# VectorE's order in the expert stage of a decoder layer: the copy of a step's results stands elsewhere in its loop

## The reference

```python
logits = x @ gate_w.T
topv, topi = jax.lax.top_k(logits, TOP_K)          # TOP_K = 8 of 64 experts
rw = softmax(topv)
W = zeros((N, E)).at[arange(N)[:, None], topi].set(rw)
gate, up = split(einsum('nh,eih->nei', x, gu_w))   # inner size 64
inter = silu(gate) * up
out = einsum('nei,ehi->nh', inter * W[:, :, None], dp_w)
out = out + sigmoid(x @ sh_gate1_w.T) * shared_expert(x)
x = layernorm(x + out)
```

## Time and profile before

| | |
|---|---|
| median of three runs | 1790.8 us (1788.66 to 1800.23) |
| profiled execution, its own time | 1814.37 us |
| profiled execution, its span | 1812.6 us |
| mean granted TensorE clock in it | 0.943 |
| scatters in the span | 320, 321.9 us of GpSimd |
| copies of a sparse step's results | 160, 110.2 us of VectorE |

### The profile page before, as it was taken

One profiled execution on the slowest core, in us unless ns is written; L12 is line 12 of the kernel. 1 busy time (PEld: TensorE's weight loads), 2 busy tenths in 40 slices (PEclk: granted clock), 3 DMA queues, 4 the chain that ended last, 5 costly groups with the idle time before them and its releaser, 6 DMA issues. The chain is left out here.

```text
span 1812.6 us, 34769 instructions
## 1 busy us (share of the span) xinstructions
PE 1506.2 (83%) x9744; PEld 1232.2 (68%) x9744; DVE 1258.4 (69%) x3827; ACT 685.8 (38%) x1526; POOL 1052.3 (58%) x1023
## 2 busy tenths in 40 slices
PE   4799999999999889989899864887877778777596
PEld 3687878888787778878788753565555555555454
DVE  3788888888888888888888844455555555333387
ACT  3444444343444434434353412232222332222264
POOL 3557666676767667667676742555555555555421
PEclk8899999999999999999999976988899999989898
DMA  7513231322222121111211394655555655554596
GB/s 260 160 56 103 81 105 67 109 75 94 90 87 99 47 77 51 66 65 46 75 53 64 91 307 139 201 174 166 174 174 171 187 170 177 173 162 141 210 419 272
DMA packets 182739, 246.40 MB, mean 136 GB/s; under 512 B 30732, under 2 KB 159321, under 8 KB 178148
## 3 DMA queue, kind: packets, MB, share of 16 engines
q1 hardware_dynamic: 148948, 169.71, 30.4%
q0 software_dynamic: 27648, 69.28, 10.4%
q10 hardware_dynamic: 6032, 6.13, 1.0%
HBM read 136.19 MB, written 117.19 MB: 140 GB/s over the span
## 5 line engine op out<-in xcount | busy, mean ns | idle before, releaser
L1572 POOL DMA_INDIRECT expert_out_scratch<-y,target x320 | 321.9, 1006 | 272.5 <-DVE target L1781 98.8
L562 POOL DMA_INDIRECT slot_scratch<-xrow x256 | 259.5, 1013 | 187.6 <-DVE xrow L1185 116.1
L1631 PE MATMUL bank_g<-gu,x_turned 128*128 (+1 forms) x1408 | 211.5, 298 | 29.4 <-issue 15.7
L1789 DVE TENSOR_TENSOR inter<-silu,bank_g 128x128 f32<-128x128 f32 x176 | 50.4, 286 | 253.4 <-ACT silu L1697 213.9
L1631 PEld LDWEIGHTS bank_g<-gu,x_turned 128*128 128x128 f32 x1408 | 189.2, 209 | 45.6 <-issue 41.8
L754 PE MATMUL bank_d<-wo_w,o2t 128*128 128x256 f32 x1536 | 193.3, 286 | 2.0 <-DVE o2t L944 2.0
L1690 ACT ACTIVATE x_turned<-bank_x 128x512 f32<-128x512 f32 x176 | 105.5, 599 | 233.1 <-PE bank_x L1613 131.6
L754 PEld LDWEIGHTS bank_d<-wo_w,o2t 128*128 128x128 f32 x1536 | 187.4, 193 | 2.7 <-DVE o2t L944 2.7
L602 PE MATMUL bank_c<-wq_w,x1t 128*128 128x512 f32 x576 | 151.5, 409 | 29.3 <-DVE q_work L1027 25.3
L1650 PE MATMUL bank_y<-dp,inter_t 64*128 (+1 forms) x352 | 133.7, 463 | 46.8 <-DVE y L1798 19.4
L507 POOL TENSOR_TENSOR q_rs<-q_ve,minus_half 128x8 f32<-128x8 f32 x64 | 137.3, 2145 | 35.9 <-DVE q_ve L1016 29.6
(11 more groups left out here) (245 smaller groups left out, 3431.3 us busy)
## 6 DMA issues: line engine op xcount, KB each, us to landing
x_rows<-slot_scratch SPq DMA_DIRECT2D x320, 136.0 KB
results<-expert_out_scratch SPq DMA_DIRECT2D x32, 1024.0 KB, 8.8
slot_scratch<-zeros SPq DMA_DIRECT2D x16, 816.0 KB
dp<-in_down SPq DMA_DIRECT2D x161, 64.0 KB
slot_scratch<-zeros SPq DMA_DIRECT2D x8, 1088.0 KB, 9.4
gu<-in_gate_up SPq DMA_DIRECT2D x11, 768.0 KB
expert_out_scratch<-y,target POOLq DMA_INDIRECT x320
token_row_scratch<-xrow SPq DMA_DIRECT2D x32, 136.0 KB
```

The costliest lines, as they stand in the source:

```text
L562: nc.gpsimd.indirect_dma_start(out=slot_d[:, :], out_offset=bass.IndirectOffsetOnAxis(ap=xrow[slot][:, SLOT8 + k:SLOT8 + k + 1].bitcast(U3 ...
L1572: nc.gpsimd.indirect_dma_start(out=y_d[:, :], out_offset=bass.IndirectOffsetOnAxis(ap=target[n % 8][:, j:j + 1], axis=0), in_=y[s % 4][:, ...
L1631: mm = nc.tensor.matmul(bank_g[:, s % 2, j * P:(j + 1) * P], xt[s % 2][:, j, c, :], w, start=(c == 0), stop=(c == C - 1))
```

## The change

In VectorE's loop, `copy_y` is called with s-4 ahead of `match_row(s)`, and no longer with s-3 between `name_row(s)` and `bound_row(s)`. The loop has one iteration more, so that the last step's copy is still issued. Nothing else differs.

```diff
-            for s in range(STEPS + 3):
+            for s in range(STEPS + 4):
                 now = s < STEPS and sparse(s)
                 if now and number(s) == 0:
                     table_slots()
+                if 0 <= s - 4 < STEPS:
+                    copy_y(s - 4)
                 if now:
                     match_row(s)
                 if 0 <= s - 1 < STEPS:
                     gate_inner(s - 1)
                 if now:
                     name_row(s)
-                if 0 <= s - 3 < STEPS:
-                    copy_y(s - 3)
                 if now:
                     bound_row(s)
                 n = number(s) - 24 if now else None
                 if now and 0 <= n < 3 * TILES:
                     find_weights(n)
```

## The result

The changed kernel took 1811.9 us (median of six runs, 1810.3 to 1817.0); the kernel before, run beside it, took 1794.7 (six runs, 1788.7 to 1800.2). The ratio is 1.009 [1.0064, 1.0115]: 0.9% slower, some 16 us, inside "within 1%" and well above the noise. Predicted were 1798 and a range of 1780 to 1822.

A forecast was written before the change was run, and what follows sets the result against it. GpSimd's burst length and number, not busy engines, set the pace. Terms 4.5 + 4.0 + 0 + 0 - 2 = 6.5 us, taken as 7 on 1790.8, gave 1798 us; own range 1789 to 1809, wider 1780 to 1822.

The forecast's parts named there:

- Point 1: Weights stretch: copies behind a late gate product start 0.84 us later, at T+0.50 (T: burst start); 18 bursts, 4.5 us.
- Point 2: Three of 21 bursts meet TensorE at half clock, so their second scatter pair splits off; 4.0 us (1.3 to 5.4).
- the hold: TensorE signals of matmuls ending from about T+2.3 in GpSimd's burst arrive together, about 1.05 us after its last scatter.
- the rival of split bursts: Late projections' signals fall under the hold in all 21 bursts; 28 us, 1819 us; chance 0.18.
- Point 5: Weights operations lengthen scatters by 0.41 us; after copies that waited for projections the new order avoids this, gaining 2 us.
- Point 3: Outside the stretch with weights, only naming's exposed end, 0.15 to 0.2 us, delays the copy, inside the slack: nothing.
- Point 4: Match, gate and name run up to 0.84 us earlier behind a copy that waited for its projection: costed at nothing.
- the rival of longer bursts: Next gate product done 0.84 us earlier, bursts grow to six scatters; 18 us faster, 1773 us; chance 0.12.
- Point 6: At the end, the last copy has one loop iteration more; the last scatters are GpSimd's backlog: nothing.
- It changes nothing: Projections have 0.40 us of slack and scatters set the pace; 1791 us, within 5 us; chance 0.20.
- slack of 0.40 us: In the usual burst, how much later a projection may end without delaying the second scatter pair at T+2.56.

## Why the prediction was right or wrong

The direction, the wide range and the reading of the order held: the copy moved later, not earlier, and past one weights operation. The forecast's own range, 1789 to 1809, did not hold by 3 us; the wider one of 1780 to 1822, which reaches into the rivals, did. The time of 1798 was 14 us low; some 4 of these are the kernel before, whose six runs have a median of 1794.7 and not 1790.8, the rest is that the medians lie 17 us apart and not 7.

**Point 1, copy later: the times were right up to the projection.** After a late gate product the copy starts at T+0.46 (in one burst of 13 at T+0.70), predicted T+0.50. The projection was to end at T+2.13 and the second pair to start at T+3.00. In 4 of the 13 such bursts it was so (ends at T+1.99 to T+2.12, pairs at T+2.97 to T+2.99). In the other nine the projection ended at T+2.32 to T+2.75 and the pair started at T+3.19 to T+3.62. The term sized too small is the clock: eight of the nine ran their projection at half clock, where point 2 counts three such bursts. TensorE had been idle before it for 1.3 to 1.5 us, waiting for the copy; but in the four others it had been idle for 1.2 to 1.4 us too and ran at full clock (last matmul 0.38 us). The granted clock fell from the higher level to the lower at T+1.2 to T+1.6 in the eight, just before or under the projection, and at T+2.0 to T+2.7, behind it or with its end, in three of the four (in the last not within 4 us). So the longer idle time goes with the slower clock, and does not by itself decide it. Over the stretch the last matmul took over 0.40 us in 20 of 104 projections, in 14 of 103 before.

Point 1 also has it that a copy that waits for its projection does not start later. Many of these did start later: of the stretch's 96 copies, 51 started within 0.35 us of their projection's end before, 30 after. So the delay reached more copies than the 21 that were priced.

**Point 2, splits: wrong in number and in price.** Not 3 but 10 of these bursts had two scatters, and GpSimd's stretch has 20 pauses of 0.5 to 1.3 us where it had none. The price was 1.34 us each, from a pair by itself in the earlier trace rows. But in the burst above the projection at T+2.61 was not held: GpSimd had just stopped, the signal came 0.87 us before the pair, and the pause was 0.81. The next steps' signals came at once too, and four steps took 13.60 us, as before. A split cost nothing there, and the other runs of three bursts for four steps took 13.66 to 13.74 us; the hold ended with the burst, as read; what I missed is that a late projection itself ends the burst. The same fact speaks against the price of the rival of split bursts, though its condition, past T+2.3, was met in most.

**The step that failed** is therefore the sum's frame: points 1 and 2 priced bursts behind a late gate product, and those break about even; 7.4 of the 9.9 us lie at the eight shared steps, which neither the forecast nor a rival mentions. That the range held is luck of bounds and not of reading: the sum had 8.5 us for both points and 2 less for point 5, 6.5 us; measured were 9.9 with 4.8 us less of scatter time in them, so everything but the scatters' own time came to 14.7. On the other occasion the pauses at the same eight places were 9.5 to 9.7 us longer, with a loss of 5 to 6 us in all, and the experiment that leaves the weights behind the copy got them back. That is shown there. For the held occasion the table of pauses is one profile of each kernel, the pauses outside the stretch grew nearly as much each, and no experiment ran in it: what lengthened the pauses there stays open.

**Point 3, outside the stretch: right.** The copy starts at T-0.14, 0.19 later, and the second pair at T+2.55 as before.

**Point 4, the earlier gate product: right at nothing** as far as the stage shows: bursts of six fell from 7 to 2 in the steps with weights, where the rival of longer bursts needed more.

**Point 5, the longer scatters: right in kind, twice the size.** Scatters over 1.05 us went from 28 to 14 and scatter time in the stretch fell by 4.8 us, predicted 2 with a bound of 4. Twelve of the 14 are a burst's first; 8 of the 13 bursts behind a late gate product have one, two of three, as predicted. The Trainium skill (SBUF - State Buffer, Who interferes with whom) has it that a VectorE instruction with two SBUF inputs contends with a GpSimd instruction that reads SBUF, and that a tensor_reduce never does. The trace agrees: 1.39 us for the scatter where a multiplication or comparison of lines 1820 and 1825 had begun 0.14 us before it, 0.97 where a reduction had. Its price for the second pairs, 0.41 each, was mostly hidden, since these waited for the projection until T+3.48 anyway; in the three bursts whose projection was in time, it gave the T+2.97 that it would.

**Point 6, the end: right.** From the last scatter's end to the span's end it is 108.6 us, 109.2 before.

**"It changes nothing"** was nearly right on the later occasion, at 0.2 to 0.3%, and probably for another reason than its slack of 0.40 us, which belongs to held signals: there GpSimd is the bound, and what TensorE is ahead of it hides most of a late copy.

## What to carry to other kernels

When work is put ahead of an operation, look not only at the usual step but at the steps in which the bound engine gets nothing to do: in every profile of the changed kernel its pauses grew there. Before pricing a stall by its length in one burst, count a whole period of the pattern in the trace, since a split that looks costly can be paid back by the next pause. And read what the wait for a free buffer says: many such waits mean that the copies come early, before a buffer is free, and so have time to lose. Their loss from one kernel to the next warns but is no price: the changed kernel kept 5 of 47 and lost 0.2 to 0.3%, the kernel with a spare operation behind the copy kept 7 and lost nothing.

## What the runs showed of the hardware

The same kernel took 1794.7 us on one occasion and 1628 to 1632 in three later sets, with durations unchanged: a scatter 0.97 us, a copy 0.68 or 0.69. Of the 189 us between the two profiled executions, 150 lie in the expert stage and 39 ahead of it. The difference goes with signals of TensorE that come 1 to 4 us late while GpSimd issues scatters back to back: 55% of 704 with none within 0.5 us, against 4 to 5%. (A trace doesn't hold every signal, so these shares are upper bounds; the waits below don't depend on it.) SiLU's wait for gate matmuls shows it, as groups of the stretch in the kernel before, on the held occasion and on the later one:

```profile
L1697 ACT ACTIVATE silu<-bank_g 128x128 f32<-128x128 f32 x100 | 28.1, 281 | 100.4 <-PE bank_g L1631 73.6 <-remote 18.3 <-issue 8.0
```

```profile
L1697 ACT ACTIVATE silu<-bank_g 128x128 f32<-128x128 f32 x103 | 28.5, 277 | 46.0 <-PE bank_g L1631 44.3 <-issue 1.7
```

It does not follow VectorE's order, GpSimd's scatters (189 in the stretch both times) or the pacing, since all of these ran without it. Whether the chip or the occasion makes it stays open, since the first chip is not on record, and so does whether the change would cost 0.9% wherever signals are held.
